# Decoder block on one core: layer 0's softmax denominators copied out of PSUM by ScalarE and inverted in four pieces, next pair's keys and values in steady slots

## What is computed

```python
q = (x @ Wq).reshape(B, Nq, HEADS, DIM_HEAD)
k = (context @ Wk).reshape(B, context.shape[1], HEADS, DIM_HEAD)
v = (context @ Wv).reshape(B, context.shape[1], HEADS, DIM_HEAD)
sim = jnp.einsum('bihd,bjhd->bhij', q, k) * SCALE
attn = jax.nn.softmax(sim, axis=-1)
out = jnp.einsum('bhij,bjhd->bihd', attn, v)
return out.reshape(B, Nq, HEADS * DIM_HEAD) @ Wo + bo
```

## Time and profile before

| | |
|---|---|
| median of three executions | 1652.2 us |
| the profiled execution | 1652.16 us |
| its span in the trace | 1650.4 us |
| mean granted TensorE clock | 0.964 |
| PE busy | 1529.6 us (93%) |
| DVE busy | 1286.7 us (78%) |
| ACT busy | 1121.7 us (68%) |
| POOL busy | 499.5 us (30%) |

### The profile page before, as it was taken

The page is one execution under the profiler, slowest core; times in us unless marked ns, Lnnn a source line. Parts: engine busy times, 40 slices in busy tenths (PEclk is TensorE's granted clock), DMA queues, the critical chain, the costliest instruction groups (busy, mean ns, idle before and its releaser), DMA issues.

```text
span 1650.4 us, 26960 instructions
## 1 busy us (share of the span) xinstructions
PE 1529.6 (93%) x9041; PEld 550.3 (33%) x9058; DVE 1286.7 (78%) x2305; ACT 1121.7 (68%) x1534; POOL 499.5 (30%) x488
## 2 busy tenths in 40 slices
PE   6879999999999999999999998899997979999986
PEld 4312223333333333333332333344443622222223
DVE  6898988778887778887789898877775666787766
ACT  6777777767877767877767786655554459676543
POOL 6303343434533434434400010244541012233200
PEclk9759999999999999999999999999999979999998
DMA  4000000000100000000010000111110000000000
GB/s 133 7 1 6 1 1 1 1 1 17 51 1 1 2 1 3 1 1 11 20 34 1 1 1 4 47 48 43 48 29 1 1 1 1 1 1 1 1 14 13
DMA packets 14833, 22.78 MB, mean 14 GB/s; under 512 B 1990, under 2 KB 11766, under 8 KB 14710
## 3 DMA queue, kind: packets, MB, share of 16 engines
q1 hardware_dynamic: 14710, 21.22, 4.5%
HBM read 20.69 MB, written 0.52 MB: 13 GB/s over the span
## 4 chain that ended last, share of the span: by engine, by line
PE 66%; issue 12%; DVE 11%; ACT 5%; POOL 5%; DMA 0%; POOLq 0%; DVEq 0%; ACTq 0%; SPq 0%
PE PS L2143 21%; PE PS L2129 14%; PE PS L2484 6%; POOL WRK L726 5%; PE PS L2175 5%; DVE KNB L1366 3%; PE PS L2471 3%; PE PS L1996 2%; PE PS L1988 2%; PE PS L2092 2%; DVE WRK L1416 2%; PE PS L2513 2%; ACT KNB L945 1%; DVE QS L1422 1%; PE PS L2423 1%
## 5 line engine op out<-in xcount | busy, mean ns | idle before, releaser
L1366 DVE CUSTOM_DVE_ANT_0 KNB<-PS,KNB 128x512 f16<-128x512 f32 (+2 forms) x500 | 338.4, 689 | 159.9 <-PE PS L2175 114.9
L1416 DVE TENSOR_TENSOR WRK<-WRK 128x768 f32<-128x768 f32 (+3 forms) x400 | 426.6, 1067 | 14.4 <-ACT WRK L925 7.2
L925 ACT ACTIVATE WRK<-PS 128x1024 f32<-128x1024 f32 (+1 forms) x408 | 400.6, 1022 | 51.8 <-PE PS L2129 44.6
L700 POOL TENSOR_TENSOR WRK<-WRK 128x256 f32<-128x256 f32 x300 | 282.0, 940 | 397.6 <-ACT WRK L925 395.6
L2143 PE MATMUL PS<-WRK,V 128*64 128x512 f32 (+1 forms) x1632 | 395.6, 605 | 0.0
L945 ACT ACTIVATE KNB<-PS 128x512 f16<-128x512 f32 (+2 forms) x306 | 181.0, 591 | 99.3 <-PE PS L2175 99.2
L2317 PE MATMUL PS<-WRK,KNB 128*128 128x512 f16 x828 | 189.4, 383 | 7.4 <-POOL WRK L726 2.7
L2143 PEld LDWEIGHTS PS<-WRK,V 128*64 128x64 f32 (+1 forms) x1632 | 99.1, 136 | 194.1 <-issue 158.3
L2129 PE MATMUL PS<-KNB,KB 64*128 64x512 f16 (+1 forms) x1224 | 156.0, 377 | 0.0
L2129 PE MATMUL PS<-Q,KB 64*128 64x512 f16 (+1 forms) x1224 | 152.6, 377 | 0.0
L1146 ACT ACTIVATE WRK<-PS 128x1024 f32<-128x1024 f32 x100 | 102.3, 1024 | 51.3 <-PE PS L2471 47.8
(11 more groups left out here) (377 smaller groups left out, 1822.9 us busy)
## 6 DMA issues: line engine op xcount, KB each, us to landing
V<-in_moe_w_dram SPq DMA_DIRECT2D x44, 192.0 KB, 2.4
KNB<-in_ctx_fm_dram SPq DMA_DIRECT2D x6, 384.0 KB, 8.5
X<-in_ctx_fm_dram SPq DMA_DIRECT2D x12, 192.0 KB, 2.4
CTX<-in_ctx_fm_dram SPq DMA_DIRECT2D x6, 384.0 KB, 3.9
BW<-in_bit_w_dram SPq DMA_DIRECT2D x1, 960.0 KB, 9.2
PWK<-in_pair_w_dram SPq DMA_DIRECT2D x4, 192.0 KB, 2.6
XT<-in_x_fm_dram SPq DMA_DIRECT2D x1, 512.0 KB, 4.8
X<-in_x_tm_dram SPq DMA_DIRECT2D x1, 512.0 KB, 11.8
```

The lines of the kernel that those rows point to most:

```text
L700: e.tensor_tensor(total, total, part, ALU.add).then_inc(S("acc_pool"), 1)
L925: e.activation(PR[0:r, u % 2, b, :], bank(2 * b, 2 * b + 2, slice(0, r)), ACT.Exp).then_inc(S("exp"), 1)
L1366: return e.tensor_tensor_reduce(diffs, sums, diffs, 0.5, NEG, ALU.add, ALU.max, accum_out=out)
L1416: e.tensor_tensor(total, total, part, ALU.add).then_inc(S("acc"), 1)
```

## The change

The denominators' way out of PSUM is split. ACT copies bank 5 to SBUF (`DEN1`, the free upper half of `QS`) in the slot of `den`, and bank 5 counts as freed by that copy. DVE takes the reciprocals from SBUF in four pieces of 128 columns, each in a slot of its own: for the half before, `den` is in slot 3, the pieces in 5, 7, 8 and 10, `norm` in 13 and `wo` in 15; for the pair's first half they are in 28, then 30, 34, 38 and 42, then 43 and 46. The next pair's keys go to slots 27, 29, ... 51 and its values to 28, 30, ... 50, one item to a slot. SP's loads of the context for pair 1's reductions are moved ahead of its load of the output weights, which waits for `wo`. Two semaphores of POOL become one. The last half (7) keeps the old reciprocals.

```diff
--- before.py
+++ after.py
@@ -119,13 +119,17 @@
     at = {s: [] for s in range(SLOTS + 1)}
     if p:
         at[3].append(("den", 2 * p - 1))
-        at[4].append(("den2", 2 * p - 1))
-        at[5].append(("wo", 2 * p - 1))
+        for k, s in enumerate((5, 7, 8, 10)):
+            at[s].append(("rec", (2 * p - 1, k)))
+        at[13].append(("norm", 2 * p - 1))
+        at[15].append(("wo", 2 * p - 1))
     if p == 0:
         at[12].append(("bits", 0))
-    at[27].append(("den", 2 * p))
-    at[28].append(("den2", 2 * p))
-    at[29].append(("wo", 2 * p))
+    at[28].append(("den", 2 * p))
+    for k, s in enumerate((30, 34, 38, 42)):
+        at[s].append(("rec", (2 * p, k)))
+    at[43].append(("norm", 2 * p))
+    at[46].append(("wo", 2 * p))
     if p + 1 < PAIRS:
         n = p + 1
         at[0] += [("wk", n), ("q", (n, 0)), ("q", (n, 1))]
@@ -133,12 +137,9 @@
         for c in range(1, NMC):
             at[4 + 3 * c].append(("kd", (n, c)))
             at[5 + 3 * c].append(("ks", (n, c)))
-        early = [("dk", 0, 30), ("v", 0, 30), ("dk", 1, 31), ("dk", 2, 32), ("v", 1, 32), ("dk", 3, 33), ("v", 2, 33)]
-        for kind, c, s in early:
-            at[s].append((kind, (n, c)))
-        for c in range(4, NKP):
+        for c in range(NKP):
             at[NU + 2 * c + 1].append(("dk", (n, c)))
-        for g in range(3, NVG - 1):
+        for g in range(NVG - 1):
             at[NU + 2 * g + 2].append(("v", (n, g)))
     if p:
         at[0].append(("v", (p, NVG - 1)))
@@ -146,7 +147,7 @@
 
 
 ITEMS = [items_of(p) for p in range(PAIRS)]
-FREED_BY = {"v": "v_ev", "q": "q_lo", "kd": "k16", "ks": "k16", "dk": "k_lo", "den": "den_r", "wo": "r_add",
+FREED_BY = {"v": "v_ev", "q": "q_lo", "kd": "k16", "ks": "k16", "dk": "k_lo", "den": "den_cp", "wo": "r_add",
             "bits": "bit_dve"}
 BANK_OF = {("q", 0): 6, ("q", 1): 7, ("kd", 0): 6, ("ks", 0): 7}
 
@@ -456,7 +457,7 @@
         RMR0 = PS[:, 2, 416:416 + 2 * NT]
         RMS = KG[1][:, T:T + 2 * NT]
         RMD = KG[1][:, T + 32:T + 32 + 2 * NT]
-        DEN2 = QS[:, 0:HALF]
+        DEN2, DEN1 = QS[:, 0:HALF], QS[:, HALF:T]
         RW_TM = [None]
 
         HB_ = BIG[:, KT * HD:2 * KT * HD]
@@ -566,6 +567,12 @@
                     q.wait_ge(S("wk_lo"), p + 1)
                     q.wait_ge(S("wv_lo"), p + 1)
                     q.dma_start(PWK[:, :, :], pair_w[p + 1, :, 0:3, :]).then_inc(S("ld_pwk"), 16)
+                if p == 1:
+                    q.wait_ge(S("r_bias"), 1)
+                    for c, (a, w) in enumerate(KP):
+                        if c:
+                            q.wait_ge(S("axp"), c)
+                        q.dma_start(XC[:, 0:w], ctx_fm[:, a:a + w]).then_inc(S("ld_cx"), 16)
                 if p and p + 1 < PAIRS:
                     q.wait_ge(S("r_add"), 2 * p)
                 if p + 1 == PAIRS:
@@ -575,12 +582,6 @@
                         q.dma_start(CTX[0:DC, a:a + w], ctx_fm[:, a:a + w]).then_inc(S(f"ld_ctx{c}"), 16)
                     q.wait_ge(S("r_add"), 2 * p)
                 q.dma_start(PWO[:, :], pair_w[p, :, 3, :]).then_inc(S("ld_pwo"), 16)
-                if p == 1:
-                    q.wait_ge(S("r_bias"), 1)
-                    for c, (a, w) in enumerate(KP):
-                        if c:
-                            q.wait_ge(S("axp"), c)
-                        q.dma_start(XC[:, 0:w], ctx_fm[:, a:a + w]).then_inc(S("ld_cx"), 16)
             q.wait_ge(S("x_fm"), 4)
             q.wait_ge(S("moe_zero"), 1)
             for h in range(2):
@@ -710,11 +711,11 @@
             w3 = SWAP.rearrange("p (a b) -> p a b", b=2)
             diag(w3[:, :, 1], 0, 1.0, [[-2, D // 2]])
             diag(w3[:, :, 0], -1, -1.0, [[-2, D // 2]])
-            e.sem_inc(S("swap"), 1)
+            e.sem_inc(S("masks"), 1)
             link(e.memset(DUP, 0.0))
             for base in (0, HD, -HD):
                 diag(DUP, base)
-            e.sem_inc(S("dup"), 1)
+            e.sem_inc(S("masks"), 1)
             for r in range(2):
                 link(e.tensor_scalar(BT1[:, r:r + 1], sm(f"b_att{r}"), 0.1, None, ALU.mult))
             e.wait_ge(S("ln_x"), 2 * NT)
@@ -924,6 +925,12 @@
                         e.wait_ge(S("acc_pool"), tile_no(hf2, i2, min(b, tiles_of(i2)[-1])) + 1)
                 e.activation(PR[0:r, u % 2, b, :], bank(2 * b, 2 * b + 2, slice(0, r)), ACT.Exp).then_inc(S("exp"), 1)
 
+            def denominators_out(hf):
+
+                e.wait_ge(S("den_ps"), hf + 1)
+                e.wait_ge(S("den_r"), hf)
+                e.activation(DEN1, bank(5), ACT.Copy).then_inc(S("den_cp"), 1)
+
             def copy_out(hf):
 
                 e.wait_ge(S("pv"), unit_no(hf, NU - 1) + 1)
@@ -955,6 +962,8 @@
                     q_out(*a, bank_of(x))
                 elif kind in ("kd", "ks"):
                     k16_out(*a, int(kind == "ks"), bank_of(x))
+                elif kind == "den":
+                    denominators_out(a)
                 elif kind == "dk":
                     k_out(*a, 5)
                 elif kind == "v":
@@ -1423,6 +1432,15 @@
                 if k:
                     ins.then_inc(S("den_r"), 1)
 
+            def quarter_of_reciprocals(hf, k):
+
+                part = slice(k * P, (k + 1) * P)
+                e.wait_ge(S("den_cp"), hf + 1)
+                e.wait_ge(S("on"), hf)
+                ins = e.reciprocal(DEN2[:, part], DEN1[:, part])
+                if k == 3:
+                    ins.then_inc(S("den_r"), 1)
+
             def normalize(hf):
 
                 e.wait_ge(S("den_r"), hf + 1)
@@ -1465,10 +1483,9 @@
                     q_out(*a, bank_of(x))
                 elif kind == "dk":
                     k_out(*a, 5)
-                elif kind == "den":
-                    reciprocals(a, 0)
-                elif kind == "den2":
-                    reciprocals(a, 1)
+                elif kind == "rec":
+                    quarter_of_reciprocals(*a)
+                elif kind == "norm":
                     normalize(a)
                 elif kind == "wo":
                     add_out(a)
@@ -1621,7 +1638,7 @@
 
 
             e.wait_ge(S("rot_sd"), 1)
-            e.wait_ge(S("swap"), 1)
+            e.wait_ge(S("masks"), 1)
             link(e.reciprocal(GR, GD))
             link(e.tensor_tensor(G3, sm("rot").rearrange("p (a b) -> p a b", b=2),
                                  GR.unsqueeze(2).to_broadcast([P, 3, 2]), ALU.mult))
@@ -2440,7 +2457,7 @@
                 ins = e.matmul(bank(h), BQ[:, 256:384], XQ[:, h * HALF:(h + 1) * HALF], start=True, stop=True)
             ins.then_inc(S("f_int"), 1)
             e.wait_ge(S("fused"), 1)
-            e.wait_ge(S("dup"), 1)
+            e.wait_ge(S("masks"), 2)
             for h in range(2):
                 ins = e.matmul(bank(h), DUP, XT[:, h * HALF:(h + 1) * HALF], start=True, stop=True)
             ins.then_inc(S("f2_ps"), 1)
```

## The result

The changed kernel took 1642.7 us (median of six executions, 1641.1 to 1644.0), the kernel before beside it 1652.2 (six, 1649.7 to 1656.5): a ratio of 0.9939 [0.9926, 0.9953], 9.5 us less, 0.6%. The range of 1641.0 to 1649.8 held it. The forecast of 1646.1 was 3.4 us too high, and the class that came out, faster by over 0.5%, had a chance of 0.31 against 0.63 for the class next to it; the interval reaches from 0.47% to 0.74%, so that the bound of 0.5% was passed isn't certain.

The account below looks back on a forecast made before the run. PE was taken to bound these stages, with DVE on the path only where reciprocals and normalization come in two slots; -11.0 + 2.3 + 0.6 + 0.5 + 1.5 = -6.1 us from 1652.2 gave 1646.1 us, range 1641.0 to 1649.8.

Parts of the forecast that it names:

- The gain: PE's waits for DVE's lumped reciprocals and normalization, and pair 3's projection waits for reciprocals, should go: 11.0 us.
- The five events: Halves 0 to 4, slots 3 to 5 or 27 to 29: PE held up by DVE, 5 x (0.21 + 1.64) = 9.25 us.
- The losses: New waits in keys slots and behind pieces or normalization, booked at 2.3, 0.6, 0.5 and 1.5 us.
- (b): Slot 5, pairs 1 and 2: piece without other item makes the next last step 0.3 us late, 0.6 us for both.
- (c): Pair 1, slots 10 and 13: context reduction beside a piece or the normalization, 0.3 and 0.2, together 0.5 us.
- (d): Slot 43, pairs 0 to 2: normalization together with dk 8 delays the next last step, 3 x 0.5 = 1.5 us.
- (a): Keys just in time: dk 0 to 3 put at their limit, 4 chunks x 3 pairs x 0.19 = 2.3 us.
- At no cost: ACT's seven copies (up to 4.2 us if uncovered), moved PE matmuls, SP's loads and pair 3's DVE work: nothing counted.
- hidden waits: Rival, chance 0.30: ACT and POOL catch up, some 0.6 us of losses left, -10.4 us, 1641.8 us.
- The moved wait: Rival, chance 0.09: DVE's stall returns at the 20 pieces of pairs 0 to 2, 0.55 us each, 1652 us.
- the slower case: Rival, chance 0.06: key copies on ACT hold PE in dk 0 to 3's slots, 19.7 us, total 1663.5 us.

Follow-up runs that it names:

- two pieces: Changed kernel with two reciprocal pieces of 256 columns (slots 5 and 8, 30 and 38) instead of four of 128: 1646.1 us, ratio 0.9961.
- all covered: Changed kernel with early keys and values back in slots 30 to 33, half-before pieces in 7, 8, 13, 14, later normalizations and `wo`: 1642.7 us, ratio 0.9943.

## Why the prediction came out as it did

**The gain**: booked 11.0 us. The five events went whole: slots 3 to 5 of pair 1 took 14.91 us before and 11.96 with 1.09 of `wo` moved to slot 15, a gain of 1.86, where 1.85 was booked. Pair 3, from its first exponential to its last, took 178.6 us and takes 176.8, 1.8 less where 1.73 was booked. One thing more went that the prediction hadn't seen: pair 2's slot 43 lasted 5.02 us before and lasts 4.75. Together that is 11.4.

**The losses**: booked 4.9 us, measured 3.6. This step, the prices of (b), (c) and (d), is the one that failed, in size and not in kind.

- (a), keys just in time: 0.19 us in each of the twelve slots, 2.3 us, as booked. PE's timeline of pair 0's slot 27, changed kernel, has the 2.06 us of dk 4's slot before:

```profile
245.27 1.94 PE L2160 MATMUL PS<-WRK,V 128*64 128x512 f32 x8
247.33 0.39 PE L2192 MATMUL PS<-KNB,Q 64*128 64x512 f16 x2
```

- (b), slot 6: 0.3 booked, 0.18 measured, twice. The order was right (POOL first); the size wasn't, as I let DVE's sum take 0.87 us behind POOL's end, and the maximum came 0.74 behind it. In the other two cases shown it is 0.73 and 0.74.
- (c): 0.3 and 0.2 booked for slots 10 and 13; 0.14 came, in slot 11, and nothing behind slot 13.
- (d), slot 44: 0.5 booked, 0.27 measured, three times. I had the list's order wrong: `norm` is put into it before the keys, so DVE does it before the low part. In the order that I priced, the run gave 0.63 (5.11 against 4.48), where my upper end said 0.9; the same 0.14 accounts for half of the difference.

**At no cost**: ACT's copy is hidden (0.35 us for doing it twice). `wo`, SP's loads and pair 3 added no wait. The piece takes 0.947 us from SBUF against 0.966 for the PSUM row, and the next instruction starts 0.87 behind it where 0.89 was booked. The Trainium skill, "VectorE: DVE Perf Modes", section on the TRN2 errata, says that DVE's instructions from SBUF pay a fixed extra latency each. That is an extra against the specification, not against PSUM, and against PSUM none shows here: 256 columns took 1.747 us from SBUF (two pieces) and 1.740 from PSUM in the same profile. A fixed part of each instruction does show, 2 x 0.947 - 1.747 = 0.15 us, half of it hidden by the neighbour: four pieces occupy DVE for 4 x 0.87 = 3.5 us a half, two of 256 columns for 2 x 1.66 = 3.3.

**The sum**: the attention gained 7.8 us where 6.1 were forecast, 1.3 of the difference from the losses and 0.4 from the gain. The other 1.7 us of the 9.5 lie outside it, in code that the change doesn't touch; in the profiles the clock came back sooner there. Half of before's executions have that shorter time too, so this part isn't shown to be the change's, and the prediction had no term for it. It is half of the 3.4 us by which the forecast was off, and it decided the class: the attention's 7.8 us alone are 0.47%, within the 0.5% to which the prediction had given 0.63. The range held the result by its width, not because this part had been seen.

**The rivals**: *hidden waits* gave 1641.8, nearest to the result, but not by its mechanism: ACT did not catch up in any of the twelve slots, and in the attention its 10.4 us are further from the 7.8 than the forecast's 6.1. *The moved wait* and *the slower case* didn't come; their mechanisms did in edits nearby: a piece ahead of a low part cost 0.44 us a pair, and keys moved with `den` and `wo` left in place 2.6.

## What to carry over

Work that stalls the bounding engine because it comes in one lump should be spread over places where that engine's own slot is longer (6.3 of the 7.8 us here), and cut finer where a part doesn't fit (1.5). Behind each place one asks two things: what stands behind it in its engine's queue, and which bank or buffer waits for that. Read the order of a list from the code before pricing it; a wrong order here was worth 0.36 us a pair. And compare the stretch that was changed, whose slots repeat to 0.01 us, before the totals: those of one kernel moved by up to 7 us, and edits that made the attention shorter had medians no lower. A few profiles of each kernel don't tell a difference from that scatter; the spans of all executions do more.

## What the runs showed that I hadn't expected

A GpSimd sum that waited while DVE ran a two-input instruction from SBUF went ahead of DVE's next one, as read from the records of one edit, in three pairs alike; DVE's was then recorded from its nominal start (1.48 us for 0.95), so a long record may be waiting. Behind such a wait only 0.73 to 0.74 us passed to the next instruction's start instead of 0.87. And identical code behind the attention took between 636.4 and 641.7 us in fourteen profiles. The changed kernel had it four times within 0.7 us, which looked like a property of the kernel; but executions of one kernel differ as much as kernels do (all covered 770.8 to 775.2 us outside the attention).
